# A graph network in three phases: bias rows placed in PSUM by ScalarE, one bank for the whole context sum

## The reference, cut to what matters

```python
u = einsum('bid,bjd->bij', h, h) / sqrt(384)
delta = softmax(u) * adjacency
attn = delta / (sum(delta, -1) + 1e-10)
hl, hs, hr = h @ Wl.T + bl, h @ Ws.T + bs, h @ Wr.T + br
ctx = (attn * upper) @ hl + diag(attn)[:, None] * hs + (attn * lower) @ hr
o = relu((ctx - mean(ctx)) / sqrt(var(ctx) + 1e-12) * gamma + beta)
# block 1: x = x + o2, where o2 is the second layer on o1;  block 2: x = x + o3
```

## Time and profile before

| | before |
|---|---|
| median of 3 runs | 1339.25 us (1338.05 to 1341.2) |
| span of the profiled execution | 1338.4 us |
| PE busy | 1301.0 us, 97%, 7818 products |
| DVE busy | 1271.9 us, 95%, 3308 |
| POOL busy | 879.6 us, 66%, 918 |
| ACT busy | 803.3 us, 60%, 1949 |
| chain that ended last | PE 62%, DVE 18%, issue 12%, POOL 3% |
| DMA | 59.20 MB, mean 44 GB/s |

### The profile page before, as it was taken

How to read it: one execution, slowest core, us unless ns; L and a number is a source line. 1 busy time by engine, 2 the same in 40 slices (tenths; PEclk the granted TensorE clock), 3 DMA queues, 4 the chain that set the end, 5 groups by cost and what they waited for, 6 DMA issues and landing times.

```text
span 1338.4 us, 29377 instructions
## 1 busy us (share of the span) xinstructions
PE 1301.0 (97%) x7818; PEld 1269.7 (95%) x7818; DVE 1271.9 (95%) x3308; ACT 803.3 (60%) x1949; POOL 879.6 (66%) x918
## 2 busy tenths in 40 slices
PE   8999999999999899999999999999999999999996
PEld 6999999999999899999999999999999999999996
DVE  7999999999999799999999999999999999999998
ACT  6666666666666555555555555566666566566663
POOL 3766666666667566666665666776776776767675
PEclk9999999999999999999999999999999999999999
DMA  5110111111011211011110110211101010101111
GB/s 170 33 47 31 47 34 45 38 40 47 31 54 32 74 48 32 31 47 31 41 38 31 47 31 32 77 50 41 39 31 47 31 47 31 47 31 44 34 45 39
DMA packets 46229, 59.20 MB, mean 44 GB/s; under 512 B 3696, under 2 KB 46192, under 8 KB 46192
## 3 DMA queue, kind: packets, MB, share of 16 engines
q1 hardware_dynamic: 46192, 58.77, 13.8%
HBM read 46.17 MB, written 12.58 MB: 44 GB/s over the span
## 4 chain that ended last, share of the span: by engine, by line
PE 62%; DVE 18%; issue 12%; POOL 3%; ACT 2%; DMA 1%; DVEq 1%; SPq 0%; ACTq 0%; POOLq 0%
PE right_bank L400 15%; PE left_bank L400 15%; PE self_bank L400 14%; PE context_bank L434 10%; DVE side_rows L708 5%; PE score_bank L374 4%; DVE context L744 3%; PE node_bank L363 3%; POOL rstd L864 2%; DVE rows L757 1%; DVE score L642 1%; DVE context L714 1%; DMA vector_rows<-vectors 1%; DVE stats L718 1%; ACT node_t L494 1%
## 5 line engine op out<-in xcount | busy, mean ns | idle before, releaser
L868 POOL TENSOR_TENSOR side_parts<-side_rows,side_parts 128x384 fp32r<-128x384 f32 x384 | 426.1, 1120 | 175.8 <-ACT side_parts L534 172.6
L400 PE MATMUL self_bank<-weight,node_t 128*128 128x384 f32 x1728 | 339.9, 340 | 0.6 <-POOL weight L887 0.4
L400 PE MATMUL right_bank<-weight,node_t 128*128 128x384 f32 x1728 | 333.2, 336 | 5.5 <-DVE side_rows L708 5.3
L400 PE MATMUL left_bank<-weight,node_t 128*128 128x384 f32 x1728 | 332.1, 335 | 0.7 <-DVE weight L693 0.7
L534 ACT ACTIVATE side_parts<-side_rows 128x384 fp32r<-128x384 f32 x384 | 191.2, 522 | 224.9 <-DVE side_rows L708 155.0
L400 PEld LDWEIGHTS right_bank<-weight,node_t 128*128 128x128 f32 x1728 | 301.5, 188 | 10.5 <-issue 9.8
L400 PEld LDWEIGHTS self_bank<-weight,node_t 128*128 128x128 f32 x1728 | 298.1, 188 | 1.0 <-issue 0.6
L400 PEld LDWEIGHTS left_bank<-weight,node_t 128*128 128x128 f32 x1728 | 298.1, 188 | 1.0 <-issue 1.0
L875 POOL TENSOR_TENSOR context<-self_rows,context 128x384 f32<-128x384 f32 x192 | 195.5, 1018 | 120.5 <-ACT context L549 118.3
L434 PE MATMUL context_bank<-side_parts,attn_t 128*128 128x384 f32 x1152 | 248.4, 350 | 16.3 <-issue 15.8
L434 PEld LDWEIGHTS context_bank<-side_parts,attn_t 128*128 128x128 f32 x1152 | 192.2, 188 | 22.2 <-issue 21.3
(11 more groups left out here) (56 smaller groups left out, 1726.3 us busy)
## 6 DMA issues: line engine op xcount, KB each, us to landing
rows<-x SPq DMA_DIRECT2D x32, 384.0 KB, 3.4
adj_in<-adj SPq DMA_DIRECT2D x96, 128.0 KB, 2.1
io<-x SPq DMA_DIRECT2D x32, 384.0 KB, 3.1
out<-io SPq DMA_DIRECT2D x31, 384.0 KB, 2.5
piece<-weights SPq DMA_DIRECT2D x18, 192.0 KB, 2.9
vector_rows<-vectors SPq DMA_DIRECT2D x15, 192.0 KB, 4.6
rows<-weights SPq DMA_DIRECT2D x3, 576.0 KB, 7.0
out<-io SPq DMA_DIRECT2D x2, 192.0 KB, 1.9
```

What stands on the lines that cost most here:

```text
L400: mm = nc.tensor.matmul(bank[:, 0:D], node_t[:, s.parity, k, c, a], weight[:, s.phase % 2, w, c, b], start=(c == 0 and a == b), stop=last)
L868: nc.gpsimd.tensor_tensor(side_parts[:, side, LO], side_rows[:, side], side_parts[:, side, HI].bitcast(F32), ALU.subtract).then_inc(side_l ...
```

## The change

VectorE no longer adds bias rows, and no `start` flag begins a product. ScalarE copies the bias row into the PSUM bank (`seed_side`, `seed_self`), and the nine products accumulate onto it. The SELF product goes into `context_bank[k]`, of which there are now two. ScalarE scales it there by the diagonal, in place, and `weigh` accumulates onto the result, so the bank holds the whole context; L714, L549 and L875 have no successor. ScalarE rounds the side's high part out of PSUM, and VectorE (not GpSimd) subtracts for the low part. GpSimd writes edge blocks of 512 columns with their zeros and a separate diagonal product; ScalarE's half-block copies (L518) are gone. The node transposes are issued one at a time inside `project` of RIGHT 0 and LEFT 0, phase 1's edge transposes inside SELF 0. The vector rows have two buffers, and a phase's rows are loaded three steps before it begins. The first bias rows are loaded ahead of the second x tile pair. TensorE's, ScalarE's and VectorE's orders are new.

```diff
-            def project(s, k, w, bank, done):
+            def project(s, k, w, bank, done, turned=None, edges=False):
                 for c in range(CH):
-                    for a, b in ((HI, HI), (HI, LO), (LO, HI)):
+                    for a, b in PASSES:
                         mm = nc.tensor.matmul(bank[:, 0:D], node_t[:, s.parity, k, c, a], weight[:, s.phase % 2, w, c, b],
-                                              start=(c == 0 and a == b), stop=last)
+                                              start=False, stop=(c, a) == (CH - 1, LO), skip_group_check=True)
+                        if turned is not None and (a, b) == (HI, LO):
+                            transpose_nodes(*turned, c)
+                        if edges and c < 2 and a == HI:
+                            transpose_edges(s, c, b)
...
             def weigh(s, k):
                 pe.wait_ge(attn_hi, s.n + 1)
                 pe.wait_ge(attn_lo, s.n + 1)
-                at_least(pe, context_done, s.tile(k))
+                pe.wait_ge(self_scaled, s.tile(k) + 1)
...
# TensorE's body
+                project_side(s, 0, RIGHT, turned=(nxt, 0) if nxt.exists() else None)
                 if prev.exists():
                     weigh(prev, 1)
+                project_side(s, 0, LEFT, turned=(nxt, 1) if nxt.exists() else None)
+                project_self(s, 0, edges=not s.bounded)
+                if nxt.exists():
+                    scores(nxt)
                 project_side(s, 1, RIGHT)
                 if nxt.exists():
                     turn_cross(nxt)
                 weigh(s, 0)
+                project_side(s, 1, LEFT)
                 project_self(s, 1)
...
# ScalarE
+            def seed_side(s, k, side):
+                bias_rows_here(s, k)
+                at_least(act, side_lo[side], s.tile(k))
+                nc.scalar.activation(side_bank[side][:, 0:D], vector_rows[:, s.phase % 2, ROW_LEFT + side], ACT.Copy)\
+                  .then_inc(side_seeded[side], 1)
+            def seed_self(s, k):
+                bias_rows_here(s, k)
+                at_least(act, centred, s.tile(k) - 1)
+                nc.scalar.activation(context_bank[k][:, 0:D], vector_rows[:, s.phase % 2, ROW_SELF], ACT.Copy)\
+                  .then_inc(self_seeded, 1)
...
# the end of ScalarE's body, after weigh(s, 0)
+                if after.exists():
+                    fill_source(after, 0)
+                split_side(s, 1, RIGHT)
+                if nxt.exists():
+                    exponentials(nxt)
+                    seed_side(nxt, 0, RIGHT)
                 split_side(s, 1, LEFT)
                 if nxt.exists():
+                    seed_self(nxt, 0)
                 if after.exists():
                     fill_source(after, 1)
+                if nxt.exists():
+                    seed_side(nxt, 0, LEFT)
+                scale_self(s, 1)
...
# VectorE
+            def split_side(s, k, side):
+                dve.wait_ge(side_hi[side], s.tile(k) + 1)
+                nc.vector.tensor_tensor(side_parts[:, side, LO], side_bank[side][:, 0:D],
+                                        side_parts[:, side, HI].bitcast(F32), ALU.subtract).then_inc(side_lo[side], 1)
...
# the second half of VectorE's body
                 if nxt.exists():
                     sum_scores(nxt)
                 if nxt.exists() and not nxt.bounded:
                     row_maximum(nxt)
                     shift_scores(nxt)
+                if after.exists() and after.bounded:
+                    input_shift(after)
                 if prev.exists():
                     norm(prev, 1)
+                split_side(s, 1, RIGHT)
+                context_stats(s, 0)
                 if prev.exists() and prev.phase > 0:
                     residual(prev, 1)
+                gather_moments(s, 0)
                 if nxt.exists():
                     mask_edges(nxt)
+                centre(s, 0)
+                split_side(s, 1, LEFT)
                 if nxt.exists() and nxt.bounded:
                     mask_rows(nxt)
                 if nxt.exists():
                     sum_kept(nxt)
...
# SP, ahead of the first step
             load_first(RIGHT)
+            load_bias_rows(0)
             load_x(Step(0, 0, 1))
```

More of the change, by code:

```diff
@@ L323, in body @@
                     load_piece(phase, i)
[L324 to L327, removed]
+                if s.phase == 1:
+                    load_residual(s)
+                if isinstance(s.n, int) and s.g == PAIRS - 3 and s.phase + 1 < PHASES:
+                    load_bias_rows(s.phase + 1)
+                    load_norm_rows(s.phase + 1)
                 if prev.exists() and prev.phase == 2:
@@ L432, in weigh @@
                     pe.wait_ge(side_lo[side], s.tile(k) + 1)
-                    for a, b in ((HI, HI), (HI, LO), (LO, HI)):
-                        mm = nc.tensor.matmul(context_bank[:, 0:D], attn_t[:, a, k, triangle], side_parts[:, side, b],
-                                              start=(side == RIGHT and a == b), stop=(side == LEFT and a == LO))
+                    for a, b in PASSES:
+                        mm = nc.tensor.matmul(context_bank[k][:, 0:D], attn_t[:, a, k, triangle], side_parts[:, side, b],
+                                              start=False, stop=(side == LEFT and a == LO), skip_group_check=True)
                 mm.then_inc(context_product, 1)
@@ L568, in body @@
                 split_side(s, 0, RIGHT)
+                if s.bounded:
+                    split_edges(s)
+                seed_side(s, 1, RIGHT)
                 if nxt.exists():
                     split_nodes(nxt, 1)
-                place_blocks(s)
                 split_side(s, 0, LEFT)
-                split_edges(s)
+                scale_self(s, 0)
+                if not s.bounded:
+                    split_edges(s)
+                seed_side(s, 1, LEFT)
                 if nxt.exists():
                     copy_cross(nxt)
-                scale_self(s, 0)
                 if len(pieces) > 0:
                     split_piece(*pieces[0])
-                scale_self_bias(s, 0)
+                seed_self(s, 1)
+                if after.exists():
[4 more added lines that the diff above has]
+                    seed_side(nxt, 0, RIGHT)
                 split_side(s, 1, LEFT)
-                split_side(s, 1, RIGHT)
                 if len(pieces) > 1:
@@ L600, in _ @@
             split_nodes(start, 1)
+            act.wait_ge(banks_open, 1)
+            seed_side(start, 0, RIGHT)
             split_first(RIGHT)
             copy_cross(start)
+            seed_side(start, 0, LEFT)
             split_first(LEFT)
@@ L606, in _ @@
             fill_source(start.ahead(1), 1)
+            seed_self(start, 0)
             split_first(SELF)
@@ L750, in residual @@
                 if s.phase == 1:
[L751 to L757 removed]
+                    dve.wait_ge(residual_in, 16 * (s.n + 1 - PAIRS))
+                other = residual_x[:, k:k + 1] if s.phase == 1 else rows[:, s.slot(k)]
+                nc.vector.scalar_tensor_tensor(rows[:, s.slot(k)], context[:, k:k + 1], 0.0, other, ALU.max, ALU.add).then_inc(post_done, 1)
             def body(s):
                 prev, nxt, after = s.ahead(-1), s.ahead(1), s.ahead(2)
+                denominator(s)
+                diagonal(s)
+                squared_denominator(s)
                 if after.exists() and after.bounded:
                     input_stats(after, 0)
[L763 to L773 removed]
                 if nxt.exists():
@@ L840, in _ @@
             final = Step(2, STEPS // 2 - 1, 1)
-            sum_context(final, 1)
             context_stats(final, 1)
-            centre(final, 0)
             gather_moments(final, 1)
@@ L907, in body @@
                 if nxt.exists():
-                    triangles_of(nxt)
+                    place_edges(nxt)
             pool.wait_ge(consts_set, 1)
@@ L914, in _ @@
             pool.wait_ge(triangles_in, 16)
-            triangles_of(start)
+            place_edges(start)
             walk(pool, body)
@@ L934 @@
     below = np.tril(np.ones((NODES, NODES), np.float32), -1)
-    triangles = np.stack([below.T, below, np.eye(NODES, dtype=np.float32)], axis=1)
+    empty = np.zeros_like(below)
+    own = np.eye(NODES, dtype=np.float32)
+    triangles = [np.stack(t, axis=1) for t in ([below.T, empty, below, empty, own], [empty, below.T, empty, below, own])]
     arrays = {
```

282 lines of the change are left out of this document (109 added, 173 removed).

## The result

The changed kernel takes 1349.11 us (median of 4 runs, 1348.66 to 1350.24), the one before 1338.65 beside it (4 runs, 1338.03 to 1341.2): a ratio of 1.0075, 95% interval 1.0061 to 1.0090. The forecast was 1318, range 1296 to 1337. The profiled execution has a span of 1346.6 us against 1338.4.

A forecast was written before the change was run, and what follows sets the result against it. TensorE's count of products was taken to bound phase 0; phases 1 and 2 each lost 0.6 us a step to waits. Terms summed to -21.2 on a 1338.4 us span, 1317.2, plus 0.85 to match the median: 1318, range 1296 to 1337.

The forecast's parts named there:

- steps, phase 0 (29): Phase 0's repeated steps go from 13.15 to 13.21 us: 29 x 0.06 = +1.7 us.
- steps, phase 1 (28): Phase 1's repeated steps go from 14.04 to 13.62 us: 28 x -0.42 = -11.8 us.
- steps, phase 2 (26): Phase 2's repeated steps go from 13.62 to 13.56 us: 26 x -0.06 = -1.6 us.
- ends of phases: Between phases, vector rows loaded three steps ahead leave the chain: -5.3 us at the first boundary, -3.7 at the second.
- head: Kernel start: 576 KB of bias rows go ahead of the second x pair, whose landing is on the chain: +2.0 us.
- tail: Kernel end: the last step's 1.32 us wait goes, with one sum and one `centre` behind the last product: -2.5 us.
- the new loop: Each step: `weigh(s, 1)` waits for `scale_self(s, 1)`, last on ScalarE; steps of 13.21, 13.62 and 13.56 us in phases 0, 1, 2.
- X: End of `weigh(s, 0)` to end of `scale_self(s, 1)`: 4.90, 4.87, 5.25 us in phases 0, 1, 2; bounds -0.15 and +0.30.
- TensorE's way back: From the scaling's release to the end of the next `weigh(s, 0)`: 8.31 us a step, with 0.44 more in phase 1.
- its slower rival: In each step, `scale_self(s, 1)` comes more than 0.22 us later than forecast; at +0.3, 1346 us; chance 0.10.
- Lone transposes: Node transposes issued singly between long products cost 0.11 us each, no change; rival that they are cheap: 1304 us, chance 0.06.
- Waits vanish: Rival: short ScalarE operations on PSUM and overlapping fills leave TensorE alone setting steps of 13.1, 13.5, 13.1; 1297 us, chance 0.14.

The follow-up runs named there:

- the doses in both directions: Against the changed kernel: in-place scaling moved ahead of fill and LEFT seed, 1307.70 us; ahead of that seed only, 1317.54; that seed written twice instead, 1399.06.
- all three edits: Changed kernel with scaling ahead of second fill and LEFT seed, first fill behind RIGHT 1 split, bias rows behind x: 1299.54 us, ratio 0.9704 to before.

## Why the prediction was wrong

| term | predicted us | measured us |
|---|---|---|
| steps, phase 0 (29) | +1.7 | 393.2 - 381.4 = +11.8 |
| steps, phase 1 (28) | -11.8 | 388.0 - 393.1 = -5.2 |
| steps, phase 2 (26) | -1.6 | 360.6 - 354.1 = +6.5 |
| ends of phases | -9.0 | -2.6 and -5.2, together -7.9 |
| head | +2.0 | +6.0 |
| tail | -2.5 | -2.3 |
| in none of these | 0 | -0.7 |
| sum | -21.2 | +8.2 |

The steps and ends are counted as in the forecast, from the same copies of L521 as of L529 (third, 32nd, 34th, 62nd, 68th and 94th start). The first and last steps lie outside, and the copy has another place in the step: hence the -0.7.

**The step that failed is the size of the new loop.** Its mechanism was right, item by item, and the doses in both directions prove it. But X, from the end of `weigh(s, 0)` to the end of the scaling, was priced too low in phases 0 and 2, and TensorE's way back from there to the end of the next `weigh(s, 0)` was priced too low in all three. ScalarE and VectorE in the changed kernel, phase 0, where `weigh(s, 0)` ended at 205.45:

```profile
205.29 0.71 ACT L492 ACTIVATE source<-rows,in_shift,in_rstd 128x384 f32 x1 [1.73 <-DVE in_shift L642]
205.91 0.47 ACT L538 ACTIVATE side_parts<-right_bank 128x384 fp32r<-128x384 f32 x1
206.41 0.56 DVE L719 TENSOR_TENSOR side_parts<-right_bank,side_parts 128x384 fp32r<-128x384 f32 x1 [0.72 <-ACT side_parts L538]
207.49 0.18 DVE L729 BATCH_NORM_AGGREGATE moments<-stats 128x2 f32<-128x6 f32 x1
207.68 0.29 DVE L676 TENSOR_TENSOR edge<-score,adj_in 128x128 f32<-128x128 f32 x1
207.89 0.61 DVE L743 SCALAR_TENSOR_TENSOR context<-context_bank,moments,vector_rows 128x384 f32<-128x384 f32 x1
208.53 0.50 ACT L544 ACTIVATE context_bank<-vector_rows 128x384 f32<-128x384 f32 x1 [0.63 <-DVE context L743]
208.97 0.69 ACT L492 ACTIVATE source<-rows,in_shift,in_rstd 128x384 f32 x1
209.56 0.47 ACT L532 ACTIVATE left_bank<-vector_rows 128x384 f32<-128x384 f32 x1
209.98 0.53 ACT L550 ACTIVATE context_bank<-context_bank,diag 128x384 f32<-128x384 f32 x1
```

Against the forecast (phase 0: its phase 2 times, and from the moments on 0.35 less) the starts are late by: fill 0.05, split 0.07, subtraction 0.05, statistics 0.07, moments 0.10 (2.04 against 1.94), mask 0.19, `centre` 0.14 (2.44 against 2.30), seed of SELF 0.15, fill of half 1 0.19, seed of LEFT 0.18, scaling 0.20; it ended at 5.06 against 4.90. No single price was far off: 0.07 was there at the statistics, 0.14 at `centre`, and the rest came on ScalarE behind the seed.

TensorE's way back is 1.36 to the end of `weigh(s, 1)` (210.51 to 211.87), then 1.91, 1.56, 0.71, 1.56, 0.17 and a `weigh` of 1.11: 8.38 against 8.31. Together 13.44. Steps of 13.47 and 13.60 alternate, each turn of the code's loop taking two steps. X is 5.06 in the longer one too, but there `weigh(s, 1)` starts 0.21 behind the scaling (196.89, 197.10) and not 0.05, and the way back is 8.56. So in phase 0 X and the way back share the miss about equally.

In phase 2 X was 5.43 and 5.34 in turn against 5.25: in the step with 5.43 the fill started 0.24 behind the input shift that releases it, 0.16 later than forecast, and the delay ran through to the end. The way back was 8.41 and 8.52. In phase 1 X was 4.90 against 4.87, as good as forecast, and the miss is the way back: 8.88 and 9.01 against 8.75.

None of these is large: 0.37, 0.27 and 0.27 us a step. Over the 83 steps of the forecast they are 25 us, more than the whole gain; the head adds 4.0, the ends 1.1. The prediction named this as its slower rival, at 1346 for +0.3 a step, with a chance of 0.10. Its reasons were half right: the queue was in order with the scaling last, and hand-overs cost more than none. The prices of seed and scaling were not the cause: 0.50 as taken for the seed, 0.54 in place of 0.57 for the scaling.

```profile
L532 ACT ACTIVATE right_bank<-vector_rows 128x384 f32<-128x384 f32 x192 | 95.2, 496 | 46.8 <-DVE side_parts L719 37.5
L550 ACT ACTIVATE context_bank<-context_bank,diag 128x384 f32<-128x384 f32 x192 | 104.2, 543 | 98.1 <-PE context_bank L396 98.1
```

The same scaling into SBUF took 569 ns before, so the Trainium skill ("ScalarE: Activation LUTs", section "Step-by-step: what each stage is for"), by which ScalarE writes to PSUM faster, has the sign right: 26 ns, too little to make the waits vanish.

**The head was missized.** x landed 2.0 us later, as forecast. Step 0's products ended 6.0 later: the gap that the landing left was followed by the low clock, 1.4, and the first RIGHT 0 waited for ScalarE's fill of the next step, which with the rest of the new order made 2.6. I priced the landing alone.

**What was right.** Lone transposes cost 0.11 each, as the three in the earlier trace rows did. The 56 ns of the Trainium skill ("TensorE: Matmul & The Clock Gate", section "Back-to-back issue gap") appeared neither alone nor in a group; that section calls it an isolated figure and gives about 81 ns for a stream of such products, and these transposes took longer than either. `centre` was 612 ns in the mean. VectorE, GpSimd and ScalarE ended at 81%, 25% and 64% (near 70% was forecast for ScalarE). No DMA of vector rows is left in the chain between phases. The fill held the split in phases 0 and 2 only. The idle time sits ahead of the `weigh` behind RIGHT 0. "Waits vanish" gave 13.1, 13.5 and 13.1 a step. That came only when the queue was put in order (13.14, 13.61 and 13.08 with all three edits), and not by the shorter operations on PSUM that the rival had assumed.

## What to carry to other kernels

Where a change puts a new operation between two groups of products, place it in its engine's queue by its deadline, ahead of work for later steps: here that order was worth 41 us, four times what the whole change lost. A loop whose forecast lies above TensorE's own count was here a fault to be mended in the order of the queue, not a number to be accepted. And the sum over a dozen hand-overs was some 0.3 us short; over 95 steps that is near 30 us, so the range should have reached as far on the slow side.

## What was not expected of the hardware

A product of 512 columns in full float32 into a bank took 0.87 us at the full clock, in two records. The 3.4 us without products ahead of 12.80, while x was awaited, were followed by a granted clock of 0.50 until past 20 us, though TensorE worked again from 12.8 on; three products in the gap kept it at 1.00. Of the loop's two steps one is 0.13 us longer in phase 0, because `weigh(s, 1)` starts 0.21 behind the scaling and not 0.05; what delays it was not separated.
